# Graph convolution on TensorE: the summing products written as four products of 32 targets

## The reference, cut to what matters

```python
def gcn_conv(x, W, b, src, dst, n):
    h = x @ W
    deg = jnp.zeros((n,), h.dtype).at[dst].add(1.0) + 1.0
    dinv = jax.lax.rsqrt(deg)
    norm = dinv[src] * dinv[dst]
    agg = jax.ops.segment_sum(h[src] * norm[:, None], dst, num_segments=n)
    return agg + h * (dinv * dinv)[:, None] + b
h = gcn_conv(emb, W1, b1, src, dst, NTOKEN)
nodes = gcn_conv(h, W2, b2, src, dst, NTOKEN)
return nodes[input.reshape(-1)].reshape(b_, l_, NINP)
```

## Time and profile before

| | us |
|---|---|
| median of 3 runs (2668.12 to 2671.47) | 2669.42 |
| span of the profiled execution, first to last instruction | 2692.9 |
| busy in that span: DVE | 2301.7 (85%) |
| PE products | 2076.2 (77%) |
| PE weight loads | 1728.1 (64%) |
| ACT | 1927.1 (72%) |
| POOL | 912.5 (34%) |
| first layer: first gather to last scatter | 896 to 1802 |
| second layer | 1820 to 2620 |

### The profile page before, as it was taken

How to read it: one execution, slowest core, us unless ns; L and a number is a source line. 1 busy time by engine, 2 the same in 40 slices (tenths; PEclk the granted TensorE clock), 3 DMA queues, 4 the chain that set the end, 5 groups by cost and what they waited for, 6 DMA issues and landing times.

```text
span 2692.9 us, 87734 instructions
## 1 busy us (share of the span) xinstructions
PE 2076.2 (77%) x36894; PEld 1728.1 (64%) x36895; DVE 2301.7 (85%) x3711; ACT 1927.1 (72%) x5267; POOL 912.5 (34%) x704
## 2 busy tenths in 40 slices
PE   3455555555562699899999899979999999999990
PEld 2345454444321467787777677868888888888870
DVE  9999999999988688899989999967777777777760
ACT  7869999999663886566666667756777777767760
POOL 2000000000000344435734455414233566655546
PEclk8566666665786899999999999999999999999995
DMA  4000000000021333343446455576888545545431
GB/s 115 0 1 1 1 1 1 1 1 1 19 70 43 106 117 119 123 131 111 106 116 132 120 144 143 143 198 200 245 245 243 153 141 142 142 138 142 135 109 18
DMA packets 191625, 277.10 MB, mean 103 GB/s; under 512 B 122458, under 2 KB 130538, under 8 KB 190972
## 3 DMA queue, kind: packets, MB, share of 16 engines
q1 hardware_dynamic: 168924, 244.05, 28.3%
q0 software_dynamic: 22304, 27.40, 8.4%
HBM read 219.68 MB, written 51.81 MB: 101 GB/s over the span
## 4 chain that ended last, share of the span: by engine, by line
PE 49%; DVE 35%; ACT 7%; issue 4%; POOL 2%; DMA 2%; SPq 0%; another core or an unknown queue 0%; DVEq 0%; POOLq 0%; ACTq 0%
PE ps L1366 28%; PE ps L1315 16%; DVE keys L1610 7%; DVE keys L1611 7%; DVE oh L1946 4%; DVE oh L1460 4%; DVE arena L1460 3%; ACT arena L1118 1%; ACT grow_t L1044 1%; PE ps L1341 1%; PE ps L1251 1%; DVE keys L1630 1%; DVE keys L1631 1%; ACT grow_t L1133 1%; DVE keys L1872 1%
## 5 line engine op out<-in xcount | busy, mean ns | idle before, releaser
L1133 ACT ACTIVATE grow_t<-ps 128x384 bf16<-128x384 f32 x2744 | 1143.6, 499 | 528.5 <-PE ps L1315 491.4
L1366 PE MATMUL ps<-grow_t,oh 128*128 128x192 bf16 x10952 | 1057.9, 248 | 4.7 <-issue 3.5
L1366 PEld LDWEIGHTS ps<-grow_t,oh 128*128 128x128 bf16 x10952 | 880.7, 98 | 128.3 <-issue 111.1
L1946 DVE TENSOR_TENSOR oh<-iorep,dl 128x2048 bf16<-128x2048 bf16 x686 | 832.7, 1218 | 132.4 <-PE ps L1366 103.7
L1315 PE MATMUL ps<-arena,keys 128*32 128x192 bf16 x21952 | 611.4, 249 | 65.9 <-DVE keys L1872 23.8
L1315 PEld LDWEIGHTS ps<-arena,keys 128*32 128x32 bf16 x21952 | 428.7, 97 | 201.6 <-issue 139.8
L951 POOL DMA_INDIRECT zring<-table,sidx x296 | 383.9, 1297 | 497.6 <-PE ps L1315 446.0
L859 POOL DMA_INDIRECT arena<-line,row_i x22 | 29.8, 1354 | 832.1 <-DVEq L1688 825.6
L1044 ACT ACTIVATE grow_t<-colf,arena 128x128 bf16<-128x128 f32 x992 | 294.3, 393 | 7.7 <-PE ps L1179 7.7
L1872 DVE TENSOR_SCALAR keys<-keys,rowf 128x2048 bf16<-128x2048 int16 x344 | 259.7, 755 | 30.3 <-DMA keys<-srel 20.2
L1610 DVE TENSOR_TENSOR keys<-keys 128x1280 f32<-128x1280 f32 (+4 forms) x212 | 246.6, 1163 | 12.6 <-ACT keys L1097 9.4
(11 more groups left out here) (246 smaller groups left out, 1915.0 us busy)
## 6 DMA issues: line engine op xcount, KB each, us to landing
keys<-srel SPq DMA_DIRECT2D x344, 512.0 KB
out<-res SPq DMA_DIRECT2D x50, 512.0 KB
table<-arena SPq DMA_DIRECT2D x19, 384.0 KB, 2.8
table<-sgn_l SPq DMA_DIRECT2D x73, 96.0 KB
arena<-table SPq DMA_DIRECT2D x5, 960.0 KB, 8.5
zring<-table,sidx POOLq DMA_INDIRECT x296
nodes<-arena SPq DMA_DIRECT2D x73, 64.0 KB
arena<-in_L_rec_edge_index SPq DMA_DIRECT2D x2, 1171.5 KB, 5.3
```

Of the source, the lines that this page charges most:

```text
L1133: act.activation(grow[:, (layer * NB + j) % DEEP, h * 2 * ROW:(h + 1) * 2 * ROW], psum[HALF_BANK[layer][HB * j + h][0]][:, 0:2 * ROW], ACT ...
L1366: mm = pe.matmul(sums(sl, k), dwin[:, (layer * NB + j) % DEEP, t // TT, k * P:(k + 1) * P, t % TT], grow[:, (layer * NB + j) % DEEP, t * R ...
L1946: dve.tensor_tensor(dwin[:, (layer * NB + j) % DEEP, 0:made[1], :, :], iorep[:, :, :].unsqueeze(1).to_broadcast(made), dl_h[:, j * BT:j * ...
```

## The change

Each summing product of the layers is written as four products. Each of the four has 32 of the 128 weight columns and writes the 32 PSUM partitions that belong to them; the moving operand is the same for all four. That holds for the scatter, for the surplus lists and for the own rows (with 384 moving columns). The sums come out the same. Semaphores are raised by the last of the four.

```diff
-                def sums(sl, k):
-                    return py[sl % 2][:, k * ROW:(k + 1) * ROW]
+                def add_rows(bank, k, one_hot, rows, first, last):
+                    for q in range(WIN):
+                        mm = pe.matmul(bank[q * ROOM:(q + 1) * ROOM, k * ROW:(k + 1) * ROW], one_hot[:, q * ROOM:(q + 1) * ROOM],
+                                       rows, start=first, stop=last)
+                    return mm
...
-                    pe.matmul(py[sl % 2][:, 0:SUP * ROW], ident_h[:, :], xtab[:, b * ROW:(b + SUP) * ROW], start=True, stop=False)
+                    for q in range(WIN):
+                        pe.matmul(py[sl % 2][q * ROOM:(q + 1) * ROOM, 0:SUP * ROW], ident_h[:, q * ROOM:(q + 1) * ROOM],
+                                  xtab[:, b * ROW:(b + SUP) * ROW], start=True, stop=False)
...
                             for k in range(SUP):
-                                mm = pe.matmul(sums(blk, k), ooh[:, out_of[item], k * P:(k + 1) * P], zring[:, u, :],
-                                               start=False, stop=False)
+                                mm = add_rows(py[blk % 2], k, ooh[:, out_of[item], k * P:(k + 1) * P], zring[:, u, :], False, False)
...
-                                mm = pe.matmul(pt[:, k * ROW:(k + 1) * ROW], ooh[:, out_of[mini[n]], k * P:(k + 1) * P], zring[:, u, :],
-                                               start=(n == 0), stop=(n == 1))
+                                mm = add_rows(pt, k, ooh[:, out_of[mini[n]], k * P:(k + 1) * P], zring[:, u, :], n == 0, n == 1)
...
                     for k in range(SUP):
-                        mm = pe.matmul(sums(sl, k), dwin[:, (layer * NB + j) % DEEP, t // TT, k * P:(k + 1) * P, t % TT],
-                                       grow[:, (layer * NB + j) % DEEP, t * ROW:(t + 1) * ROW],
-                                       start=False, stop=(w == CELLS - 1 and k == SUP - 1))
+                        mm = add_rows(py[sl % 2], k, dwin[:, (layer * NB + j) % DEEP, t // TT, k * P:(k + 1) * P, t % TT],
+                                      grow[:, (layer * NB + j) % DEEP, t * ROW:(t + 1) * ROW],
+                                      False, w == CELLS - 1 and k == SUP - 1)
```

## The result

| | before | after |
|---|---|---|
| median of the runs (4 each), us | 2670.44 (2668.12 to 2673.24) | 3309.47 (3297.81 to 3315.52) |
| ratio, 95% interval | | 1.2391 [1.2365, 1.2417] |
| span of the profiled execution, us | 2692.9 | 3313.6 |
| first layer, first gather to last product, us | 906 | 1128 |
| second layer, the same, us | 800.3 | 1207.6 |

I had forecast 2577 with a range of 2548 to 2650. The two layers account for all of it: 222 + 407 = 629 us, less 8 us of a shorter pause between them, is the 621 us between the two spans. This is rival A, the feed of instructions, to which I had given 0.16.

A forecast was written before the change was run, and what follows sets the result against it. TensorE's stream was taken to bound the second layer, DVE the first with TensorE a close second. Savings of 75 us (second layer borders) and 17 us (first layer) sum to 92: 2669.4 - 92 = 2577 us, range 2548 to 2650.

The forecast's parts named there:

- rival A: TensorE's instruction feed too slow for 192 instead of 96 a batch; 2790 us at 13 ns each; chance 0.16.
- border of form: TensorE's switch between 32-column gathers and full products: 0.11 us lost each, 0.22 a batch, 75 us saved in second layer.
- a four of the scatter: Four 32-column summing products on four quarters, taken as 82.5 ns like the gathers' fours; bounds 80 to 330 ns.
- own rows and surplus: Products beside the scatter, written as fours: same cost as before, 0.16 and 0.17 us, and no border added.
- start-to-start floor of about 25 ns: Skill rule against the change: a four 100 ns, a batch 2.4 us, second layer some 69 us slower; trace disagreed.
- Batch: (8 + 16) x 82.5 = 1.98 us: Second-layer batch as 8 gather fours and 16 scatter fours of 82.5 ns: 1.98 us instead of 2.20.
- the break-even of 11.5: 2.20 us / 192 instructions: a feed slower than 11.5 ns each makes the second layer slower than before.
- nothing in the bursts shows a slower second half: Argument against a slow instruction feed: TensorE's bursts, such as 64 in 0.66 us, keep their pace.
- the longest run without pause: 128 loads and products at the layer's start in 2.5 us, 20 ns each; says only that the feed holds 20.
- 690 / 2.25 is 307 batches: Batch count in 690 us of the second layer, matched with 282 and 256 idle weight loads, about one per border direction.
- Well over 3500: Kernel time in us if the feed took 20 ns an instruction, 3.84 us a batch.
- The first layer: DVE holds the pace, TensorE a close second; only DVE's waits for TensorE shrink: 17 us, bounds 0 to 36.

The follow-up runs named there:

- 6: Kernel before, second layer: gathers and scatters alternate one half at a time, 8 borders a batch instead of 2, same instructions; 2916.29 us, 1.0802 of before.
- the signals: Kernel before with one or two semaphore increments nobody waits for behind each summing product of the second layer; 1.0762 and 1.3883 of before.
- small loads: Changed kernel with output fills and source-list loads cut to a fraction of their bytes; 3198.84 us, 1.1849 of before.
- six halves: Kernel before, second layer gathers six halves, then scatters six, instead of four and four, same instructions; 1.0016 and, repeated, 1.0012 of before.
- 2: Kernel before with each summing product split into two of 64 targets, 128 instructions a batch; 2831.84 us, 1.0515 of before.
- 4: Kernel before, second layer: each full summing product cut into two of 96 moving columns, 128 instructions a batch; 2779.78 us, 1.0308 of before.
- experiment 1: Changed kernel, scatter's products move only 64 of 192 gathered columns, same number of instructions; 3359.35 us, 1.2465 of before.

## Why the prediction was wrong

**What held.** That the second layer is TensorE's stream and nothing else; that 0.11 us is lost at each border of form (6); that a four of the scatter takes 82.5 ns, with its weight columns two elements apart, and that own rows and surplus cost what they did (the chain of after). DVE was no obstacle: it waits for PE 336.7 us in the layer. The Trainium skill's start-to-start floor of about 25 ns (TensorE: Matmul & The Clock Gate, "Wait — 56ns, not 53.3ns?") does not hold for fours on separate quarters, neither for gathers nor for scatters: 32 in 0.66 us are 20.6 ns each.

**What failed** is the step "Batch: (8 + 16) x 82.5 = 1.98 us": the instructions that it needs do not arrive at that pace, and with the stops and the slow clock a batch of the second layer took 1207 / 343 = 3.52 us. It multiplies the pace of a burst by a length that no row of before had at that pace. A batch is 192 instructions in it, and 1.98 us are 10.3 ns each. What I had in hand: 64 in 0.66 us, a quarter of a packet; 128 loads and products at 20 ns, half a packet; 24 ns over 100 us. None of the fast ones reached across the 256 at which the stream now stops. The same rows had the answer to the question that I put aside. The earlier trace rows gave 6 us a packet, and rival A said that it would become 2.6; what was missing is the look at how close two packets ever stand. In before's second layer that is 3.49 us, and it was there to be read in the start times: 256 instructions in 3.49 us are 13.6 ns, above the break-even of 11.5. It would have been a warning and no proof, since TensorE used a packet only every 5.9 us there and seldom needed the next one sooner. The sentence "nothing in the bursts shows a slower second half" was true, and no evidence. Nor were 128 instructions "the longest run without pause": the stream of the earlier trace rows has hardly a pause in 100 us, at 24 ns; they were the longest at 20.

A small slip did not matter: "690 / 2.25 is 307 batches" should be 690 / 2.33 (800 us for 343 batches), 296.

**The rival's price** was low too: 13 ns an instruction, where the layer had 17.5, since I took a value just beyond the break-even. The average round is 4.0 to 4.5 us, not the shortest one. "Well over 3500" at 20 ns shows the right order, and 17.5 put in gives the 398 us above.

**The first layer** was to give 17 us and cost 222: TensorE was a close second there, at 2.64 us a batch, and the feed's 4.18 us a packet is 3.14 us for 192 instructions.

The Trainium skill has a rule on just this (Runtime: NRT & Kernel Launch, Instruction fetch mechanics): the sequencer fetches blocks of 16 KB, 256 instructions, ahead of itself, and the fetch is hidden since instructions are dispatched slower than it fills. The first half agrees with the traces, with stops at every 256 instructions. The second half they contradict for TensorE: loads and products are taken from the queue every 10.3 ns, and a block comes at best every 3.24 us, 12.7 ns an instruction. The page also gives TensorE room for 2048 instructions; no run here shows so deep a cover. Ahead of after's second layer TensorE stood still for 9.7 us, and yet no packet started from 6.2 us before the layer's first product to 5.5 us behind it; the first stop of the feed came after 202 products, 404 instructions.

The runs in which no other cause was put in make one rising curve, packets of the second layer and its length: 133 packets 802 us, 156 857, 176 to 179 879 to 897, 270 1180 to 1226. The array's work shrinks or stays along it. Off the curve are the runs with another cause of their own: borders by half (133, 1020), the signals (154 and 176, 1005 and 1848), and small loads (270, 1081).

**Open:** why an average round is 4.0 to 4.5 us when the shortest is 3.24; what the stops of 0.6 to 0.7 us are, which are a quarter of the stopped time of after's second layer on one chip and hardly there on another; and what keeps the next packet from starting before TensorE has resumed. No kernel here beats the one before: the 0.22 us a batch of the borders is real, but both ways to it bring new stops, in the fours for the most part the feed's, in the six halves of a cause that is not shown.

## What to carry to other kernels

Count the instructions that an edit adds to an engine's queue, and hold them against the closest distance of its instruction packets, not against a burst: here TensorE was fed one load or product in 15.6 to 17.6 ns on average (4.0 to 4.5 us for 256), and with one in 17.2 ns (2, 4) the layer was already 10% longer, so that an edit that saves array time by more instructions has to stay well above that. The pace of a short run is shown for a run as long as the longest in the trace, and no longer. A stop that the profile calls "issue", and that recurs after the same number of instructions whatever line it falls on, points to the feed.

## What the runs showed of the hardware

- Instructions come in packets of 16 KB, 256 instructions. TensorE resumed 2.2 to 2.75 us after the start of a packet (0.96 us long); two packets started at least 3.24 us apart in after's layers (3.22 in those of experiment 1), on average 4.5 us in its second layer, and 4.0 with most of the other traffic gone. A pause of 9.7 us left no more than 404 instructions in store.
- A change between 32-column and 128-column (or 64-column) products costs 0.105 to 0.11 us in each direction.
- Four 32-column products of 192 moving columns on four quarters take 82.5 ns, and with 64 moving columns in the scatter's fours the layer took the same 1207 us (1).
- Signals on TensorE's queue, with or without a load and a product between them, follow each other every 151 ns (9), though each is recorded with 51.
- The 1.2 GHz stretches of after's second layer (188 us at a granted clock of 0.50) hold 2.8 us of the 403 us of stops, and packets stand no further apart there. A layer at a granted clock of 0.82 (1) and one at 0.92 both took 1207 us.
